# Attention weighed by pairs of heads with split operands, and a router on raw rows

## The chip, the cores and the metric

One core of one Trainium2 chip runs the whole program. The metric is the device time of one execution in microseconds (us). Its engines: TensorE (PE, with its weight loads as PEld), VectorE (DVE), ScalarE (ACT), GpSimd (POOL) and SyncE (SP, which here only issues transfers). They run their own instruction streams in order and meet at semaphores. SBUF is the working memory; PSUM, eight banks of 128 partitions x 512 fp32 values, takes the results of PE.

## The reference, cut to what matters

Four sequences of 256 rows of 256 values go through four sublayers, each added to its input:

```
x = x + graph_attention(ctx, adjacency = layernorm(x))      # 2 layers, 8 heads
x = x + sparse_mixture(layernorm(x))                        # 8 experts, top 2
x = x + learned_adjacency(ctx, layernorm(x))                # similarity, top 76 a row
x = x + block(x)                                            # below

# block: 32 query heads on 4 key/value heads of 128, then 32 experts (top 8) and a shared one
q, k, v = rope(h @ Wq), rope(h @ Wk), h @ Wv                # h = rmsnorm(x) * ln1
attn    = softmax(causal(q @ k.T / sqrt(128)))
x       = x + (attn @ v) @ Wo
x       = x + experts(rmsnorm(x) * ln2)

# router of the sparse mixture
logits = layernorm(x) @ w_router                            # 1024 rows x 8
weights, chosen = top_2(softmax(logits))
```

The change touches `attn @ v` and the router of the sparse mixture.

## The kernel before

Activations lie as eight tiles of 128 rows; a sequence is two of them. The stages follow one another on each engine: graph attention, router and ranking, sparse mixture over 23 tiles of 128 slots, learned adjacency, attention, expert mixture. Each engine's order is written out by hand; semaphores (`S[...]`) tie them.

**Attention.** 32 heads are taken in 8 blocks: block `blk` is key/value group `g = blk // 2` on one half (512 rows, two sequences). A block has ten projection jobs (values, keys, eight query heads), each 512 columns wide, at fixed iterations (`JOB_AT`), and 16 units: one query head of one sequence. Unit `u` is head `r`, sequence `b2` of `unit_of(u)`. Every engine runs `for k in range(FIRST, END)`, and in iteration `k` does its part for units at fixed lags:

- PE: `turn(k-2)`, three 128x128 transposes of the probabilities into `PT_BANK` (one bank); `scores(k+1)`; a job of `project` if there is one; `weigh(k-3)`, values times transposed probabilities into `O_BANK` (one bank), in fp32, 256 and 128 columns; `project_out(k-5)`, six fp32r products of 256 columns.
- ACT: `high_out(k-4)`, the rounded upper part of the weighed outputs into `o_ring`; `swap_halves` for the job of iteration `k-1`; `copy_T(k-2)`, from `PT_BANK` to `probT`; `exps(k)`; in some iterations upper parts of weights.
- DVE: `shift(k)` (mask and row minimum), `low_out(k-4)` (the remainder of the outputs), `normalise(k-1)`, `rotate` for the job of `k-2`, `cosines` for the job of `k-1` (for a values job: the copy to `vt`), and, from k = 6 to 13, `residual`. At k = 3 it splits the second half of the activations.
- POOL: the sine part of the rotation, lower parts of weights.

A product of two fp32 operands in *split* form is three fp32r products: upper x upper, upper x lower, lower x upper (`split_product`, L54). The projections and the output product are made so; the product with the values is not. An fp32 product shows as two records in the trace, an fp32r product as one.

**Router.** In the last iterations of the graph stage (`ALL` = 64, `LAST` = 77), for each sequence b: PE transposes the layer's output (`turn_x1`), DVE adds it to `xs` (`add_x1`) and takes mean and variance (`measure`), POOL makes the inverse root (`inverse`), DVE normalises into `norm` (`normalise_graph`), PE transposes that (`turn_graph`), ACT copies it to `actT` (`copy_graph`), PE multiplies with `wr0` into bank 2 (`route_graph`). `router0` on DVE then takes the row maximum, ACT the exponential, DVE the sum, the two largest of eight and the choice, over all eight tiles at once; PE counts ranks (`rank_slots`). SP stores the normalised rows to `x_rows` (`store_graph`), from which POOL gathers rows for the experts.

Of the kernel before, what the change touches and what calls it, by code (L numbers as in the profile page):

```python
# [14 lines left out]
P = 128  # L15
# [85 lines left out]
def build(nc, x, ctxT, W0, W1, a_self0, a_neigh0, a_self1, a_neigh1, b01,  # L101
          w_router, w_gate, w_up, w_down, WqT, WkT, gamma, ln1, ln2, Wq, Wk, Wv, Wo, Wr, ebias,
          Wg, Wu, Wd, ident_in, ind_in, rope_q, rope_k, causal_in, before_in, out):
    with ExitStack() as ctx:
# [12 lines left out]
        kv = sb("kv", [P, 2, B * N])  # L117
# [26 lines left out]
        route = sb("route", [P, 6, T, E1])  # L144
# [10 lines left out]
        kT = kv[:, 0, :]  # L155
        vt = kv[:, 1, :].rearrange("p (t n) -> p t n", t=T)
# [115 lines left out]
        def sb_resting(name, shape):  # L272
# [18 lines left out]
        probT = sb("probT", [P, 2, 3 * P])  # L291
# [6 lines left out]
        down_w = sb("down_w", [P, 2, I1 // P, D])  # L298

# [13 lines left out]

            "chosen_done", "earlier_done", "count_ready", "owner_done", "hot_done", "kind_done", "put_done", "place_done", "idx_ready", "idx_done", "rows_out",
# [18 lines left out]
            "s_ready", "s_shift", "p_exp", "p_inv", "p_norm", "pT_ready", "pT_copied",  # L333
# [16 lines left out]
        NORM_AT, TURN_AT, ROUTE_AT = (ALL, ALL + 2, ALL + 10), (ALL + 2, ALL + 4, ALL + 11), (ALL + 4, ALL + 6, ALL + 12)  # L350
# [34 lines left out]

        BLOCKS = 2 * KV
# [15 lines left out]

        def turn2_bank(t):

            return (Q_BANK[0], Q_BANK[1], bank[1], bank[3])[t // 2][:, t % 2 * D:t % 2 * D + D]
# [5 lines left out]
        def unit_of(u):  # L411

            blk, rem = divmod(u, BU)
            return (blk, blk // 2, blk % 2) + divmod(rem, 2)
# [34 lines left out]
        def _(sp):  # L449
# [107 lines left out]
        def _(pe):  # L557
# [25 lines left out]
            def graph_attention():  # L583
# [99 lines left out]
                def turn_graph(b):  # L683

                    pe.wait_ge(S["norm_done"], NT * b + NT)
# [4 lines left out]
                    for nt in range(NT):  # L690
                        for c in range(HC):
                            mm = pe.transpose(MISC[:, nt * D + c * P:nt * D + c * P + P],
                                              norm[:, NT * b + nt, c * P:c * P + P], ident[:])
                    mm.then_inc(S["normT_ready"], NT)

                def route_graph(b):

                    pe.wait_ge(S["normT_copied"], NT * b + NT)
                    if b == 0:
                        pe.wait_ge(S["const_in"], 16 * 5)  # L700
                        pe.wait_ge(S["z_copied"], ALL)
                    for t in range(NT * b, NT * b + NT):
                        for c in range(HC):
                            mm = pe.matmul(bank[2][:, t * E0:(t + 1) * E0], actT[:, c, t * P:t * P + P],
                                           wr0[:, c, :], start=c == 0, stop=c == HC - 1)
# [7 lines left out]
                for k in range(-1, LAST):  # L713
# [16 lines left out]
                    for b in range(B - 1):  # L730
                        if k == TURN_AT[b]:
                            turn_graph(b)
                        if k == ROUTE_AT[b]:
                            route_graph(b)
                turn_graph(B - 1)
# [1463 lines left out]
```

## Time and profile before

| | us |
|---|---|
| median of 3 runs | 1094.86 (1094.78 to 1096.74) |
| the profiled execution | 1095.35 |
| its span | 1093.5 |
| PE busy in the span | 1001.4 (92%) |
| PEld, DVE, ACT, POOL busy | 863.9, 870.9, 640.0, 431.6 |
| mean granted clock of PE | 0.945 of full speed |
| graph stage and router | about 0 to 192 |
| sparse mixture | about 206 to 338 |
| attention | about 366 to 830 |
| expert mixture | about 830 to 1093 |

The profile is of one execution. Matmuls are pipelined: a record's duration is longer than the time by which it holds up the next, so the distance between the ends of neighbouring records is the cost of one. The same holds for DVE and ACT, where the distance between starts is the cost and the duration tells when the result is there. A row of a timeline gives the start, the duration, engine, line, operation, output and inputs, and in brackets the idle time before it and what ended it. "By line" in the chain of waits is the share of the window that each line has in the chain that ended last.

### The profile page before, as it was taken

The page shows a single profiled execution, that of the slowest core. Times are in us where ns is not written, and L with a number is a line of the kernel's source. Part 1 is how long each engine was busy: PE and PEld are TensorE (multiplying, and loading weights), DVE is VectorE, ACT ScalarE, POOL GpSimd, SP SyncE. Part 2 cuts the span into 40 slices and gives each one's busy share as a digit, 9 for nine tenths or more (in the row PEclk, how much of TensorE's full clock was granted, in tenths as well). Part 3 has the DMA queues.
Part 4 walks back from the last instruction along what each step waited for, and adds up shares of the span by engine and source line. Part 5 has one row for each costly group of instructions (what it writes and reads, how often), then busy time and mean ns, then how long its engine had stood idle before and what let it go on. Part 6 is the DMA issues. An engine that isn't in the chain of part 4 may idle for free.

```text
span 1093.5 us, 21079 instructions
## 1 busy us (share of the span) xinstructions
PE 1001.4 (92%) x6394; PEld 863.9 (79%) x6394; DVE 870.9 (80%) x2644; ACT 640.0 (59%) x1767; POOL 431.6 (39%) x372
## 2 busy tenths in 40 slices
PE   4798777999994689999999999999989999999997
PEld 2455545799993478999999999999878888888886
DVE  6999997677765889777786777777878878788887
ACT  4789984655552387877777777777843222222221
POOL 5789893543321243323232333212422332232231
PEclk9869887699997599999999999999999999999999
DMA  9700003011115011010101100000000111111111
GB/s 291 256 1 2 1 2 108 29 55 49 47 37 172 2 39 50 1 40 2 49 2 39 35 2 2 1 2 1 26 20 30 44 43 58 43 43 49 52 43 38
DMA packets 49462, 49.30 MB, mean 45 GB/s; under 512 B 4896, under 2 KB 42464, under 8 KB 49376
## 3 DMA queue, kind: packets, MB, share of 16 engines
q1 hardware_dynamic: 45888, 40.83, 11.9%
q0 software_dynamic: 2208, 6.03, 1.9%
q10 hardware_dynamic: 1280, 1.38, 0.4%
q8 instruction: 43, 0.70, 0.3%
q14 instruction: 43, 0.35, 0.1%
HBM read 43.11 MB, written 5.11 MB: 44 GB/s over the span
## 4 chain that ended last, share of the span: by engine, by line
PE 72%; DVE 11%; POOL 7%; ACT 5%; issue 4%; DMA 1%; SPq 0%; DVEq 0%; ACTq 0%; POOLq 0%
PE bank L57 13%; PE bank L58 13%; PE bank L59 13%; PE bank L954 7%; PE bank L975 5%; PE bank L857 4%; PE bank L866 4%; PE bank L878 4%; PE bank L964 3%; POOL rest L1418 3%; PE bank L976 2%; POOL alpha L1421 2%; DVE alpha L1626 1%; PE bank L646 1%; PE bank L933 1%
## 5 line engine op out<-in xcount | busy, mean ns | idle before, releaser
L1483 POOL TENSOR_TENSOR rot_s<-swap,rq 128x512 f32<-128x512 f32 x64 | 88.6, 1385 | 194.7 <-ACT swap L1261 194.6
L1134 ACT ACTIVATE silu<-bank 128x512 f32<-128x512 f32 x66 | 39.4, 598 | 173.6 <-PE bank L59 173.6
L2073 DVE TENSOR_TENSOR o_ring<-bank,o_ring 128x256 fp32r<-128x256 f32 x128 | 54.2, 424 | 80.3 <-ACT o_ring L1290 78.9
L1274 ACT ACTIVATE prob<-prob,pmin 128x128 f32<-128x128 f32 (+1 forms) x256 | 113.3, 447 | 5.5 <-DVE pmin L2054 5.5
L954 PE MATMUL bank<-kv,norm 128*128 128x128 f32 (+1 forms) x512 | 105.8, 330 | 5.2 <-DVE norm L2047 5.2
L1896 DVE SCALAR_TENSOR_TENSOR xs<-bank,wt,xs 128x256 f32<-128x256 f32 x264 | 109.0, 476 | 0.1
L1439 POOL TENSOR_TENSOR gate_r<-gate_w,gate_r 128x256 fp32r<-128x256 f32 x31 | 36.4, 1174 | 177.3 <-ACT gate_r L1127 177.3
L1290 ACT ACTIVATE o_ring<-bank 128x256 fp32r<-128x256 f32 x128 | 48.3, 377 | 76.4 <-PE bank L976 76.3
L57 PE MATMUL bank<-wo_r,o_ring 128*128 128x256 f32 x256 | 82.4, 322 | 0.0
L1874 DVE TENSOR_TENSOR hidf<-silu,bank 128x512 f32<-128x512 f32 x66 | 45.4, 687 | 44.9 <-ACT silu L1134 43.3
L2066 DVE TENSOR_SCALAR prob<-prob,pinv 128x128 f32<-128x128 f32 (+1 forms) x256 | 77.0, 343 | 4.6
L2054 DVE CUSTOM_DVE_ANT_0 prob<-bank,causal 128x128 f32<-128x128 f32 (+1 forms) x256 | 80.1, 350 | 0.1
L975 PE MATMUL bank<-probT,kv 128*128 128x256 f32 x256 | 76.9, 382 | 3.3 <-DVE o_ring L2073 3.3
L1066 ACT ACTIVATE alpha<-alpha,edge_min 128x256 f32<-128x256 f32 x128 | 64.8, 527 | 19.1 <-DVE edge_min L1626 11.9
L57 PE MATMUL bank<-actT_r,wqk_r 128*128 128x512 f32 x144 | 72.3, 502 | 3.2 <-DVE kv L2020 3.2
L57 PE MATMUL bank<-down_r,hidT 128*128 128x256 f32 x248 | 70.2, 283 | 2.7 <-DVE xs L1896 1.4
L954 PEld LDWEIGHTS bank<-kv,norm 128*128 128x128 f32 x512 | 67.7, 193 | 6.2 <-DVE norm L2047 6.1
L59 PE MATMUL bank<-wo_r,o_ring 128*128 128x256 f32 x256 | 72.2, 282 | 0.0
L58 PE MATMUL bank<-wo_r,o_ring 128*128 128x256 f32 x256 | 72.0, 281 | 0.0
L1626 DVE CUSTOM_DVE_ANT_0 alpha<-alpha,norm 128x256 f32<-128x256 f32 x128 | 69.7, 580 | 2.6 <-POOL alpha L1421 2.2
L1284 ACT ACTIVATE probT<-bank 128x384 f32<-128x384 f32 x128 | 62.7, 490 | 13.7 <-PE bank L964 7.9
L59 PE MATMUL bank<-down_r,hidT 128*128 128x256 f32 x248 | 70.2, 283 | 0.0
(309 smaller groups left out, 3151.4 us busy)
## 6 DMA issues: line engine op xcount, KB each, us to landing
gate_w<-in_Wg SPq DMA_DIRECT2D x33, 128.0 KB, 2.2
up_w<-in_Wu SPq DMA_DIRECT2D x33, 128.0 KB, 2.3
down_w<-in_Wd SPq DMA_DIRECT2D x33, 128.0 KB, 2.3
w_all<-in_w_gate SPq DMA_DIRECT2D x8, 512.0 KB, 10.6
w_all<-in_w_up SPq DMA_DIRECT2D x8, 512.0 KB, 10.4
w_all<-in_w_down SPq DMA_DIRECT2D x8, 512.0 KB, 10.6
wq_g<-in_Wq SPq DMA_DIRECT2D x4, 1024.0 KB, 5.6
wo_g<-in_Wo SPq DMA_DIRECT2D x4, 1024.0 KB, 5.6
```

Source lines behind the costliest of these rows:

```text
L57: pe.matmul(out, lhs[0], rhs[0], start=first, stop=False)
L58: pe.matmul(out, lhs[0], rhs[1], start=False, stop=False)
L59: return pe.matmul(out, lhs[1], rhs[0], start=False, stop=last)
L954: mm = pe.matmul(S_BANK[u % 2][:, nt * P:nt * P + (nt + 1) * P], qT[:, (u // 2) % 4, b2 * N + nt * P:b2 * N + nt * P + P], kT[:, b * N:b * ...
L975: pe.matmul(O_BANK[:, 0:N], vt[:, t, :], probT[:, u % 2, 0:N], start=True, stop=False)
L1066: ins = act.activation(alpha[:, k % RING, nt * N:nt * N + N], alpha[:, k % RING, nt * N:nt * N + N], ACT.Exp, bias=edge_min[:, k % RING, n ...
L1274: ins = act.activation(prob[:, u % 4, nt * P:nt * P + (nt + 1) * P], prob[:, u % 4, nt * P:nt * P + (nt + 1) * P], ACT.Exp, bias=pmin[:, u ...
L1483: pool.tensor_tensor(rot_s[:, m % 2].rearrange("p (b n) -> p b n", b=2), swap[:, m % 2].rearrange("p (b n) -> p b n", b=2), bcast(tab[:, 1 ...
L1626: ins = dve.tensor_tensor_reduce(out=alpha[:, k % RING, nt * N:nt * N + N], in0=alpha[:, k % RING, nt * N:nt * N + N], in1=adj[:, r % B, n ...
L1896: ins = dve.scalar_tensor_tensor(xs[:, t, :], DB[2 * (mod % 2) + j // 2][:, j % 2 * D:j % 2 * D + D], w, xs[:, t, :], ALU.mult, ALU.add)
L2054: ins = dve.tensor_tensor_reduce(out=prob[:, u % 4, nt * P:nt * P + (nt + 1) * P], in0=S_BANK[u % 2][:, nt * P:nt * P + (nt + 1) * P], in1 ...
L2066: ins = dve.tensor_scalar(prob[:, u % 4, nt * P:nt * P + (nt + 1) * P], prob[:, u % 4, nt * P:nt * P + (nt + 1) * P], pinv[:, u % 4, nt:nt ...
```

## The change

**Attention.** `vt` and `probT` become fp32r, with the remainders `vt_low` and `probT_low` beside them. `unit_of` is reordered so that units 2p and 2p+1 are two heads of one sequence, which share their values. `weigh` takes a pair: three products of 512 columns (both heads, first 128 keys) and three of 256 (second 128 keys, rows 128 to 255 of both), all into the one `O_BANK`. It stands at the head of even iterations. DVE gets `low_T`, which reads `PT_BANK` again; `turn` waits for that instead of the copy. `high_out` and `low_out` take a pair each, in even iterations.

**Router.** PE transposes the raw rows `xs` and multiplies them with `wr0`, from which its column means have been subtracted (`router_means`, `wr_centred`); DVE multiplies the logits by the inverse deviation (`scaled_logits`). Six tiles (`LEAD`) are routed apart from the last two, whose logits go to bank 3. The last graph's `normalise_graph` goes behind the scan in `router0`, memsets go ahead of the last `add_x1`, and SP issues the first query and value loads ahead of the last `store_graph`.

```diff
-        NORM_AT, TURN_AT, ROUTE_AT = (ALL, ALL + 2, ALL + 10), (ALL + 2, ALL + 4, ALL + 11), (ALL + 4, ALL + 6, ALL + 12)
+        NORM_AT, TURN_AT, ROUTE_AT = (ALL, ALL + 2, ALL + 10), (ALL, ALL + 1, ALL + 7), (ALL + 2, ALL + 3, ALL + 8)
 def unit_of(u):
-            return (blk, blk // 2, blk % 2) + divmod(rem, 2)
+            return blk, blk // 2, blk % 2, rem // 4 * 2 + rem % 2, rem // 2 % 2
 # SP
+            load_queries(0)
+            load_values(0)
             store_graph(B - 1)
             sp.dma_start(rq[:], rope_q).then_inc(S["att_in"], 16)
             sp.dma_start(rk[:], rope_k).then_inc(S["att_in"], 16)
-            load_queries(0)
-            load_values(0)
 # PE, graph stage
                 def turn_graph(b):
-                    pe.wait_ge(S["norm_done"], NT * b + NT)
+                    pe.wait_ge(S["x1_added"], b + 1)
 ...
-                                              norm[:, NT * b + nt, c * P:c * P + P], ident[:])
+                                              xs[:, NT * b + nt, c * P:c * P + P], ident[:])
+                def router_means():
+                    pe.wait_ge(S["const_in"], 16 * 5)
+                    pe.wait_ge(S["mean_set"], 1)
+                    pe.wait_ge(S["z_copied"], ALL)
+                    for c in range(HC):
+                        mm = pe.matmul(bank[2][:, T * E0:(T + 1) * E0], work[:, 0:P], wr0[:, c, :], start=c == 0, stop=c == HC - 1)
+                    mm.then_inc(S["wr_mean"], 1)
 # PE, attention
                 def turn(u):
                     pe.wait_ge(S["p_norm"], u + 1)
                     if u >= 1:
-                        pe.wait_ge(S["pT_copied"], u)
+                        pe.wait_ge(S["pT_low"], u)
 ...
+                def weigh(p):
+                    blk, g, half, r, b2 = unit_of(2 * p)
                     t = NT * (2 * half + b2)
+                    pe.wait_ge(S["pT_low"], 2 * p + 2)
 ...
+                    if p >= 1:
+                        pe.wait_ge(S["o_copied"], p)
+                    dst = O_BANK.rearrange("p (u n) -> p u n", u=2)
+                    for nt in range(NT):
+                        rows, cols = slice(nt * P, N), slice(nt * N, nt * P + N)
+                        for i, (v, weights) in enumerate(((vt[:, t + nt, :], probT), (vt[:, t + nt, :], probT_low),
+                                                          (v_low(t + nt), probT))):
+                            mm = pe.matmul(dst[:, :, rows], v, weights[:, :, cols],
+                                           start=nt == 0 and i == 0, stop=nt == NT - 1 and i == 2)
+                    mm.then_inc(S["o_ready"], 1)
                 for k in range(FIRST, END):
+                    if k % 2 == 0 and 0 <= k - 4 < AU:
+                        weigh((k - 4) // 2)
                     if 0 <= k - 2 < AU:
                         turn(k - 2)
 ...
-                    if 0 <= k - 3 < AU:
-                        weigh(k - 3)
 # ACT, attention
+                def high_out(p):
+                    act.wait_ge(S["o_ready"], p + 1)
+                    if 2 * p + 2 > O_RING:
+                        act.wait_ge(S["o_used"], 2 * p + 2 - O_RING)
+                    act.activation(out_pair(p, 0), O_BANK.rearrange("p (u n) -> p u n", u=2), ACT.Copy
+                                   ).then_inc(S["o_high"], 1)
                 for k in range(FIRST, END):
-                    if 0 <= k - 4 < AU:
-                        high_out(k - 4)
+                    if k % 2 == 0 and 0 <= k - 4 < AU:
+                        high_out((k - 4) // 2)
                     if (q := job_in(k, 1)) is not None:
                         swap_halves(*q)
 # ACT, router
+            act.wait_ge(S["lead_max"], 1)
+            act.activation(route[:, 0, 0:LEAD, 0:E0], route[:, 0, 0:LEAD, 0:E0], ACT.Exp).then_inc(S["lead_exp"], 1)
 # DVE, router0
+                scaled_logits(slice(0, LEAD), bank[2][:, 0:LEAD * E0], S["lead_ready"], 2 * B - 1, S["lead_max"])
+                two_largest(slice(0, LEAD), S["lead_exp"])
+                scaled_logits(slice(LEAD, T), bank[3][:, 0:NT * E0], S["logit_ready"], 2 * B, S["rmax_done"])
+                two_largest(slice(LEAD, T), S["rexp_done"])
 ...
+                normalise_graph(B - 1)
                 dve.wait_ge(S["count_ready"], 1)
 # DVE, attention
+                        dve.tensor_copy(high, src).then_inc(S["v_high"], 1)
+                        dve.wait_ge(S["v_high"], blk + 1)
+                        dve.tensor_tensor(vt_low[:, 0:4, 4 * half:4 * half + 4, :].rearrange("p j t e -> p j (t e)"),
+                                          src, high.bitcast(F32), ALU.subtract).then_inc(S["q_taken"], 1)
 ...
+                def low_T(u):
+                    dve.wait_ge(S["pT_copied"], u + 1)
+                    dve.tensor_tensor(probT_low[:, u % 2, :], PT_BANK[:, 0:3 * P], probT[:, u % 2, :].bitcast(F32),
+                                      ALU.subtract).then_inc(S["pT_low"], 1)
 ...
                 for k in range(FIRST, END):
                     if 0 <= k < AU:
                         shift(k)
-                    if 0 <= k - 4 < AU:
-                        low_out(k - 4)
                     if 0 <= k - 1 < AU:
                         normalise(k - 1)
+                    if k % 2 == 0 and 0 <= k - 4 < AU:
+                        low_out((k - 4) // 2)
+                    if 0 <= k - 2 < AU:
+                        low_T(k - 2)
                     if (q := job_in(k, 2)) is not None:
                         rotate(*q)
```

## Rows read from the trace of the kernel before

**Rows 1.** Windows: start:end, length, busy us of each engine, granted clock, DMA.
```profile
80.00:162.00 82.00, 63.91 (x514) 41.08 (x516) 79.07 (x227) 74.69 (x242) 72.63 (x47) 0.89 0.01 1
...
391.00:398.00 7.00, 4.23 (x23) 3.31 (x23) 6.03 (x15) 5.23 (x18) 1.27 (x1) 1.00 0.23 78
...
413.50:465.40 51.90, 51.09 (x328) 46.17 (x329) 45.02 (x160) 40.33 (x119) 18.00 (x14) 1.00 0.08 26
...
517.33:569.24 51.91, 51.91 (x345) 47.89 (x344) 39.32 (x150) 40.26 (x120) 18.89 (x15) 1.00 0.08 26
```
**Rows 2.** Chain of waits, one block, 517.33 to 569.24: start, us, what.
```profile
by line: PE bank L954 20.7%; PE bank L57 15.4%; PE bank L59 15.4%; PE bank L58 15.3%; PE bank L975 13.3%; PE bank L964 10.1%; PE bank L976 6.8%; PE bank L933 3.4%
...
519.12 0.43 PE bank L975 x2
520.49 0.33 PE bank L964 x3
520.82 0.66 PE bank L954 x4
521.47 0.24 PE bank L57
...
522.86 0.43 PE bank L975 x2
...
525.21 0.43 PE bank L975 x2
```
**Rows 3.** Timeline of PE: the end of a projection, the end of weighing.
```profile
538.38 0.40 PE L59 MATMUL bank<-actT_r,wqk_r 128*128 128x512 f32 x1
...
539.05 0.38 PE L976 MATMUL bank<-probT,kv 128*128 128x128 f32 x2
```
**Rows 4.** Timeline of ACT in the same iteration.
```profile
539.47 0.38 ACT L1290 ACTIVATE o_ring<-bank 128x256 fp32r<-128x256 f32 x1 [1.34 <-PE bank L976]
539.87 0.59 ACT L1260 ACTIVATE swap<-bank 64x512 f32<-64x512 f32 x1
...
541.09 0.49 ACT L1284 ACTIVATE probT<-bank 128x384 f32<-128x384 f32 x1
541.48 0.39 ACT L1274 ACTIVATE prob<-prob,pmin 128x128 f32<-128x128 f32 x1
...
542.36 0.36 ACT L1290 ACTIVATE o_ring<-bank 128x256 fp32r<-128x256 f32 x1
```
**Rows 5.** Timeline of DVE, one iteration without idle time.
```profile
535.99 0.28 DVE L2054 CUSTOM_DVE_ANT_0 prob<-bank,causal 128x128 f32<-128x128 f32 x1
...
536.66 0.42 DVE L2073 TENSOR_TENSOR o_ring<-bank,o_ring 128x256 fp32r<-128x256 f32 x1
537.00 0.15 DVE L2063 RECIPROCAL pinv<-psum_ 128x2 f32<-128x2 f32 x1
...
537.66 0.69 DVE L2047 TENSOR_TENSOR norm<-rot_c,rot_s 128x512 f32<-128x512 f32 x1
538.26 0.28 DVE L2054 CUSTOM_DVE_ANT_0 prob<-bank,causal 128x128 f32<-128x128 f32 x1
```
**Rows 6.** Timelines of ACT and PE: a wait of the transposes early in attention.
```profile
393.03 0.49 ACT L1284 ACTIVATE probT<-bank 128x384 f32<-128x384 f32 x1
...
393.66 0.52 PE L964 MATMUL bank<-ident,prob 128*128 128x128 f32 x3 [1.80 <-ACT probT L1284]
```
**Rows 7.** Chain of waits, 160 to 210: the last graph's rows and the router.
```profile
179.77 0.70 DVE xs L1667
...
183.51 1.13 PE bank L692 x4
...
187.28 0.23 DVE rcol L1727
...
191.04 0.28 DVE marks L1742
...
192.54 3.62 PE bank L561 x4
```

More of the change, by code:

```diff
@@ L1703, in graph_attention @@
                         divide(j)
+                    for b in range(B - 1):
+                        if k == NORM_AT[b]:
+                            normalise_graph(b)
                     if (j := quad_at(k, 4)) is not None:
                         elu(j)
+                    if k == ROUTE_AT[0]:
+                        dve.wait_ge(S["wr_mean"], 1)
+                        dve.tensor_tensor(wr0[:], wr0[:], bcast(bank[2][:, T * E0:(T + 1) * E0], 1, HC), ALU.subtract
+                                          ).then_inc(S["wr_centred"], 1)
                     if (r := round_at(k, 20)) is not None:
+                        if r == 2 * B - 1:
+                            dve.wait_ge(S["g_elu"], QUADS * 2 * B)
+                            dve.memset(ones[:], 1.0)
+                            dve.memset(padded[:], -1.0)
+                            dve.memset(marks[:, :, T:], 0.0)
+                            chain.link(dve.memset(same_e[:], 1.0))
+                            dve.memset(same_e[:, :, 0:1], 0.0)
                         add_x1(r)
@@ L1709, in graph_attention @@
                         measure(r)
-                    for b in range(B - 1):
-                        if k == NORM_AT[b]:
-                            normalise_graph(b)
                 measure(2 * B - 1)
-                dve.memset(ones[:], 1.0)
-                dve.memset(padded[:], -1.0)
-                chain.link(dve.memset(marks[:, :, T:], 0.0))
-                chain.link(dve.memset(same_e[:], 1.0))
-                chain.link(dve.memset(same_e[:, :, 0:1], 0.0))
-                normalise_graph(B - 1)
@@ new lines, in scaled_logits @@
+            def scaled_logits(ts, logits, ready, rms, done):
+                R = route[:, 0, ts, 0:E0]
+                dve.wait_ge(ready, 1)
+                dve.wait_ge(S["x_rms"], rms)
+                chain.link(dve.tensor_tensor(R, logits.rearrange("p (t e) -> p t e", e=E0), bcast(rstd[:, ts], 2, E0), ALU.mult))
+                chain.link(dve.tensor_reduce(rcol[:, 0, ts], R, X, ALU.max))
+                dve.tensor_tensor(R, R, bcast(rcol[:, 0, ts], 2, E0), ALU.subtract).then_inc(done, 1)
@@ L1736, in router0, with two_largest @@
+            def two_largest(ts, ready):
+                R = route[:, 0, ts, 0:E0]
+                dve.wait_ge(ready, 1)
+                chain.link(dve.tensor_reduce(rcol[:, 1, ts], R, X, ALU.add))
+                chain.link(dve.reciprocal(rcol[:, 2, ts], rcol[:, 1, ts]))
+                chain.link(dve.tensor_tensor(padded[:, ts, 0:E0], R, bcast(rcol[:, 2, ts], 2, E0), ALU.mult))
+                for t in range(ts.start, ts.stop):
                     dve.max(rtop[:, t, :], padded[:, t, 0:8])
```

100 lines of the change are left out of this document (46 added, 54 removed).

## The prediction

> **What bounds the kernel now.** I read the windows first, then the chain of waits of one steady stretch, then the timelines of the four engines in it. In the window 517.33 to 569.24, one block of 16 units of attention, TensorE (PE) is busy 51.91 of 51.91 us [rows 1]: nothing else can set the pace there. The chain of waits of that block is PE alone, and its pieces give what each step costs at the end of the pipeline, which is what a consumer sees [rows 2]. From one product with the values to the next: 3.74 us in an iteration with a projection (519.12 to 522.86), 2.35 in one without (522.86 to 525.21). Inside: three transposes 0.33, four records of scores 0.66, a projection 6 x 0.233 = 1.40, weighing 0.43 and 6.8% of 51.91/16 = 0.22, together 0.65, and the six products with the output weights what is left up to 520.49, 0.72, so 0.12 each. A block has 9 query/key jobs of 1.40 and a value job of 1.78, on iterations 1, 2, 4, 5, 7, 9 (values), 10, 12, 13, 15 counted from the block's unit 0. Taken by twos: (0,1), (2,3), (6,7), (10,11), (14,15) 6.09 each, (8,9) 6.47, (4,5) and (12,13) 7.49, sum 51.9, as the window says.
>
> The other engines have room on average, VectorE (DVE) 39.3 and ScalarE (ACT) 40.3 us [rows 1]. What matters is where they wait. ACT stands idle 1.34 us before the copy of the weighed outputs [rows 4], until the last record of L976 ends at 539.43 [rows 3], and only then swaps the halves of a projection that had ended at 538.78 [rows 3]. The swap was ready and stood behind `high_out` in ACT's order.
>
> **The change, part by part.**
>
> *Cheaper weighing.* Two units had 2 x 0.65 = 1.30 us of fp32 products. Six fp32r products take their place, three of 512 columns and three of 256. The rows give 0.233 for 512 columns of fp32r and 0.12 for 256, each with a weight load of its own [rows 2]: 3 x 0.233 + 3 x 0.12 = 1.05. Saved 0.25 a pair, 64 pairs, 16 us, if PE keeps running. If the run of 256 columns with a step between heads cost as unpipelined a record as the longest here (0.40 and 0.28), the pair would be 2.0; the nearest rows are the pipelined ones, and I take 1.05.
>
> *New DVE work.* `low_T` subtracts 384 columns out of PSUM for every unit. From start to start 256 columns take 0.34 (536.66 to 537.00) and 512 take 0.60 (537.66 to 538.26) [rows 5], so 384 take about 0.48, done after 0.57. `low_out` goes from two of 0.34 to one of 0.60, and the value job gets a second pass of 0.6 and its wait. Per block +7.7 - 0.7 + 0.7 = +7.7 on 39.3, so 47.0 below 49.9 left for PE: enough on average. In the window 413.5 to 465.4, where the residuals ride along, DVE has 45.02 already [rows 1]; with 7.7 it is over PE's 49.9 by 2.8.
>
> *Where the waits go.* This decides it. `PT_BANK` is one bank. Before, `turn(u)` waited for ACT's copy of the unit before; now it waits for `low_T`, which is behind that copy and, in even iterations, behind `low_out`. And `weigh` moves from the middle of an iteration to the head of an even one, while ACT's iteration still begins with `high_out`. So ACT reaches `high_out`, waits for a product that PE has only just begun, and behind it on ACT are the swap of the last projection (1.22 us, 539.87 to 541.09), the copy `copy_T` (0.49) and the exponentials (0.88, 541.48 to 542.36) [rows 4]. I count from the end of PE's previous iteration, for an even iteration without a projection that follows one with it (0, 6, 8, 14 of a block):
> weigh done 1.05; ACT starts 0.04 later (539.43 to 539.47) [rows 3, 4], `high_out` of 512 columns 0.60 (a swap half of 512 columns takes 0.59) to 1.70; swap to 2.92; `copy_T` done 3.41; `low_T` from 3.44 to 4.01; PE restarts 0.14 after its release (393.52 to 393.66) [rows 6] at 4.15, and three transposes from a standstill take 0.52 [rows 6]: 4.67. Then scores 0.66, projection 1.40, outputs 0.72: 7.45. Before, this pair took 6.09: +1.37 for it, and PE, whose own next piece would have been at 2.76, stands for about 1.5 us.
> Pair (2,3): the even iteration has its own projection and covers the first wait nearly (PE is through at 4.16). In the odd one ACT does exponentials to 4.19, swap to 5.41, copy to 5.90; `low_T` 5.93 to 6.50; the next weigh starts at 6.64 and, from a standstill, ends 0.24 late, so 6.88: +0.79. Pair (10,11): nothing to swap in 10, but two value passes lengthen DVE: after them `shift` (0.67), `normalise` (0.66) (535.99 to 536.66, 537.00 to 537.66) [rows 5] and `low_T` of unit 9 end at 6.09, 6.47 in all: +0.38. Pairs (4,5) and (12,13) have projections in both halves, cover everything and gain 0.25.
> A block: 4 x 1.37 + 0.79 + 0.38 - 2 x 0.25 = +6.15, so 58.1 us.
> Over the whole of attention, even iterations 4 to 120: the first kind 30 times (41.1), the second and third 7 times each (5.5, 2.7), the fourth 15 times (-3.8): +45.5. The start is bound by DVE (391 to 398: PE 4.23 of 7.00 [rows 1]): two `low_T` before the activations are split, and the first pairs, +2, between 0 and 4. The residuals add under 1 beyond what that stretch loses already. After iteration 121 there are no swaps: +1, between -1 and 3.
>
> *Router.* The last graph's rows no longer have to be measured and normalised before they are transposed: from the end of the addition at 180.46 to the transposes at 183.51 [rows 7], 3.05 us. Logits at about 184.3, not 187.28. Six tiles' routing runs on DVE meanwhile (181.55 to about 185.1), two tiles' is left, some 2.5 of the 3.76 us that eight take (187.28 to 191.04): the choice stands at 187.6, 3.4 sooner. What is next late is PE's features of the similarity (3.62 at 192.54 [rows 7]) after the ranks, which moves as a whole, since the first of the two is done while DVE chooses. The normalisation goes under the wait for the ranks. Its store goes behind the query loads on SP's queue; the gather on POOL asks for it only when DVE and PE have made the row numbers, so those hide it; without that cover it would cost the time that the store takes, about 2 us. The exponentials of ACT come twice, 0.3 us, on the path once. New memsets and the centring of the weights (under 1 us) lie beside PE's transposes. -3.3, between -4.5 and 0.
>
> *Sum.* 45.5 + 2 + 1 - 3.3 = +45.2. The profiled execution took 1095.35, its span 1093.5, so 1.85 lie around the span; it is 0.49 over the median. 1095.35 + 45.2 - 0.5 gives 1140.
>
> **A page on this.** The Trainium skill, "Perfetto Trace Analysis", section "Optimizing Tensor Performance", has two rules that pull apart here: larger matmuls are more efficient where possible, which speaks for the pair; and independent groups should rotate through PSUM banks so that emptying one overlaps the next group's products, which speaks against holding the one transposes' bank through two readers. By the first alone the sum is 16 us off; by the second the wait at that bank is what counts, as I have it.
>
> **The rivals.**
> *PE stays the bound* (12%). If ACT and DVE deliver before PE asks, only the arithmetic counts: 64 x 0.25 = 16 and 3.3 for the router, 1095 - 19 = 1076. For it: PE at 51.91 of 51.91, ACT and DVE at three quarters [rows 1]. It decides if the transposes' bank is free 2.76 us after the iteration's start; my chain has it at 4.01, so 1.25 us of it would have to be wrong, more than any one term except the swap. The same page, "Identifying the Most-Contended Engine", takes the engine of highest occupancy as the one to relieve; that rule gives this result.
> *Only the bank's wait, not the swap* (3%). If the swap got through before the copy's wait bites, the chain is 1.22 shorter, 2.79 after the start, and PE stands about 0.3 a pair from the restart alone: the 0.25 is eaten, the router remains, 1092 to 1100, say 1097.
> *The clock gives way* (5%). PE would be busy 86% of a block. In 80 to 162 it was busy 78% and was granted 0.89 [rows 1]; PE's 49.9 us a block would grow by 12%, 6 us, 45 in all: 1185. Against it: 391 to 398, with a gap of 1.80 [rows 6] and PE busy 60%, had 1.00 [rows 1].
> *The stall as worked out* (80%): 1140, by itself 1125 to 1155; 0.1 us in each of some 45 stalls is 4.5, a start or end off by its bounds 4, the router 3.
>
> **How the numbers follow.** Out of the range I leave the first rival and the clock, 17%; it takes in the second rival and the stall with all its bounds: 1096 to 1158. A measurement of this kernel tells about 0.2% from no change, 2 us: faster 0.13 (the first rival and a piece of the second), same 0.02, slower 0.85.
>
> **What would show it.** A steady block of about 58 us, not 50; PE idle before the transposes of odd units, about 1.5 us, four times a block, released by DVE's `low_T`; in each, ACT idle before `high_out`, then swap, then copy, back to back; the idle of PE at weigh smaller and rarer; (4,5) and (12,13) without gaps, 7.24 us; clock 1.00; the choice of experts 3.4 us sooner. A steady block of 50 us would prove me wrong, as would idle that ends with `p_norm` (then DVE's load is the bound, not the order on ACT).

## The result, and the profile after

The changed kernel takes 1156.26 us, the median of 4 runs (1155.75 to 1166.4), where the kernel before takes 1094.82 beside it: a ratio of 1.0574, 95% interval 1.0545 to 1.0603. It is slower by 61.4 us; the forecast said slower by 45.2. Its range ended at 1158, so the time lies just inside; the part of it that belonged to the stall alone ended at 1155. One execution of the kernel before, among those beside the first four experiments, took 4046.8 us in the slow state and counts in no ratio below. The profiled execution has a span of 1154.0 us at a mean granted clock of 0.951, so 60.5 us more than before.

Line numbers move: in the kernel after, weighing is L1009, the transposes (`turn`) L993, scores L983, `high_out` L1324, the two halves of the swap L1294 and L1295, `copy_T` L1318, `low_T` L2129, `low_out` L2134, `normalise` L2122 and `rotate` L2103.

The windows first, as in [rows 1]: one steady block of 16 units, from its values job to the next one, and a longer stretch of attention. Columns are the busy times of PE, PEld, DVE, ACT and POOL with their instruction counts, the granted clock, the DMA share and GB/s.

```profile
535.85:595.74 59.89, 52.02 (x329) 45.91 (x328) 50.66 (x159) 39.85 (x112) 18.43 (x15) 1.00 0.07 23
476.49:776.00 299.51, 260.98 (x1633) 230.63 (x1632) 247.02 (x791) 196.24 (x550) 82.76 (x65) 0.99 0.05 16
```

A block has gone from 51.91 to 59.89 us, and PE, busy all of it before, now stands for 7.9. The clock is full in that block, but not in the whole stretch, as its mean of 0.99 says:

```profile
737.00:741.00 4.00, 4.00 (x15) 3.25 (x15) 3.76 (x17) 1.13 (x5) 0.00 (x0) 0.57 0.02 6
```

It stood at the lower of its two levels (half, 1.2 GHz) from 737.3 to 740.7, after a stretch, 715 to 735, in which PE was busy 18.60 of 20.00 us. The projection's products follow one another there at 0.43 us in place of 0.23, and the pair of iterations around it takes 9.44 us where the same pair of other blocks takes 7.87. That is 1.6 us of the loss in this profile. Why the clock fell there and nowhere else in this attention after 379 us is open. What PE waits for is in the view of its waits, over the whole run (us in total, times, longest):

```profile
PE bank L993 <- DVE probT_low L2129: 47.6, 35, 1.9
PE bank L1009 <- DVE probT_low L2129: 20.3, 24, 2.4
```

Here is one stall, an even iteration without a projection after an odd one with it, first on PE:

```profile
560.48 0.39 PE L1009 MATMUL bank<-probT,vt 128*128 128x512 f32 x1
...
561.41 0.28 PE L1009 MATMUL bank<-probT,vt_low 128*128 128x256 f32 x1
561.53 0.49 PE L993 MATMUL bank<-ident,prob 128*128 128x128 f32 x3
...
563.10 0.28 PE L59 MATMUL bank<-wo_r,o_ring 128*128 128x256 f32 x1
564.80 0.52 PE L993 MATMUL bank<-ident,prob 128*128 128x128 f32 x3 [1.41 <-DVE probT_low L2129]
```

then on ACT:

```profile
561.73 0.60 ACT L1324 ACTIVATE o_ring<-bank 128x512 fp32r<-128x512 f32 x1 [1.99 <-PE bank L1009]
562.35 0.59 ACT L1294 ACTIVATE swap<-bank 64x512 f32<-64x512 f32 x1
562.96 0.59 ACT L1295 ACTIVATE swap<-bank 64x512 f32<-64x512 f32 x1
563.57 0.49 ACT L1318 ACTIVATE probT<-bank 128x384 fp32r<-128x384 f32 x1
```

and on DVE:

```profile
562.36 0.69 DVE L2134 TENSOR_TENSOR o_ring<-bank,o_ring 128x512 fp32r<-128x512 f32 x1 [0.70 <-ACT o_ring L1324]
564.09 0.56 DVE L2129 TENSOR_TENSOR probT_low<-bank,probT 128x384 fp32r<-128x384 f32 x1 [1.04 <-ACT probT L1318]
```

The zero of the forecast's chain is the end of PE's previous iteration, here 560.64 (the output product of 560.36 took 0.28). From there the weighing is done at 1.05 (561.41 + 0.28 = 561.69), `high_out` at 1.69, the swap at 2.91, the copy at 3.42, and `low_T` runs from 3.45 to 4.01; PE restarts at 4.16. The forecast had 1.05, 1.70, 2.92, 3.41, 3.44 to 4.01 and 4.15. ACT had stood for 1.99 us ahead of `high_out`, with the swap ready, and the bank that it copies last had been full since 562.02. A second finding lies in rows of another kind, DVE and then POOL at one place:

```profile
603.10 1.54 DVE L2122 TENSOR_SCALAR prob<-prob,pinv 128x128 f32<-128x128 f32 x2
```

```profile
603.02 1.28 POOL L1520 TENSOR_TENSOR rot_s<-swap,rk 128x512 f32<-128x512 f32 x1
```

The two normalisations of a unit (x2) take 0.55 us at 561.10, and 1.54 here: GpSimd's product of the sines had begun 0.08 earlier and ends at 604.30, and they end 0.34 after it. In the text below this is called a collision. `low_T`, which reads one operand from PSUM, is not held up so. The one of the stall above began at 564.09, in the middle of a product of GpSimd, and took its usual 0.56; none of the 50 that began with GpSimd at work took longer:

```profile
563.62 1.27 POOL L1520 TENSOR_TENSOR rot_s<-swap,rq 128x512 f32<-128x512 f32 x1 [6.61 <-ACT swap L1295]
```

### The profile page after: what moved, and what is told of

The parts are those of the page before. It is cut to its first block, busy times and chain, and to the rows that moved or that the text cites. A ratio compares the mean times of both kernels' runs of the same rounds, so it can differ in the third digit from the quotient of the medians.

```text
span 1154.0 us, 20728 instructions
## 1 busy us (share of the span) xinstructions
PE 998.6 (87%) x6270; PEld 847.2 (73%) x6270; DVE 947.2 (82%) x2726; ACT 636.3 (55%) x1704; POOL 427.0 (37%) x372
## 3 DMA queue, kind: packets, MB, share of 16 engines
q10 hardware_dynamic: 1280, 1.38, 0.4%
## 4 chain that ended last, share of the span: by engine, by line
PE 58%; DVE 17%; ACT 11%; issue 7%; POOL 4%; DMA 1%; SPq 0%; DVEq 0%; ACTq 0%; POOLq 0%
PE bank L57 10%; PE bank L58 10%; PE bank L59 10%; PE bank L1009 6%; PE bank L886 4%; PE bank L895 4%; PE bank L907 3%; PE bank L983 3%; DVE probT_low L2129 3%; ACT swap L1294 2%; ACT swap L1295 2%; POOL rest L1455 2%; PE bank L993 2%; ACT probT L1318 2%; DVE prob L2122 1%
## 5 line engine op out<-in xcount | busy, mean ns | idle before, releaser
L1520 POOL TENSOR_TENSOR rot_s<-swap,rq 128x512 f32<-128x512 f32 x64 | 82.3, 1287 | 246.8 <-ACT swap L1295 246.8
L983 PE MATMUL bank<-kT,norm 128*128 128x128 f32 (+1 forms) x512 | 107.0, 332 | 6.5 <-DVE norm L2103 6.5
L1324 ACT ACTIVATE o_ring<-bank 128x512 fp32r<-128x512 f32 x64 | 38.2, 597 | 125.8 <-PE bank L1009 125.8
L2129 DVE TENSOR_TENSOR probT_low<-bank,probT 128x384 fp32r<-128x384 f32 x128 | 70.7, 552 | 43.4 <-ACT probT L1318 43.4
L993 PE MATMUL bank<-ident,prob 128*128 128x128 f32 x384 | 64.2, 276 | 48.1 <-DVE probT_low L2129 47.6
L2122 DVE TENSOR_SCALAR prob<-prob,pinv 128x128 f32<-128x128 f32 (+1 forms) x256 | 89.5, 392 | 4.6
L993 PEld LDWEIGHTS bank<-ident,prob 128*128 128x128 f32 x384 | 43.0, 141 | 57.1 <-issue 57.1
L983 PEld LDWEIGHTS bank<-kT,norm 128*128 128x128 f32 x512 | 67.6, 192 | 9.0 <-DVE norm L2103 8.6
L57 PE MATMUL bank<-down_r,hidT 128*128 128x256 f32 x248 | 70.2, 283 | 3.2 <-DVE xs L1949 1.9
L2134 DVE TENSOR_TENSOR o_ring<-bank,o_ring 128x512 fp32r<-128x512 f32 x64 | 44.1, 689 | 32.4 <-ACT o_ring L1324 32.4
```

Source lines behind the costliest of these rows:

```text
L57: pe.matmul(out, lhs[0], rhs[0], start=first, stop=False)
L983: mm = pe.matmul(S_BANK[u % 2][:, nt * P:nt * P + (nt + 1) * P], qT[:, (blk * REP + r) % 4, b2 * N + nt * P:b2 * N + nt * P + P], kT[:, b ...
L993: mm = pe.transpose(PT_BANK[:, j * P:j * P + P], prob[:, u % 4, j * P:j * P + P], ident[:])
L1520: pool.tensor_tensor(rot_s[:, m % 2].rearrange("p (b n) -> p b n", b=2), swap[:, m % 2].rearrange("p (b n) -> p b n", b=2), bcast(tab[:, 1 ...
L2122: ins = dve.tensor_scalar(prob[:, u % 4, nt * P:nt * P + (nt + 1) * P], prob[:, u % 4, nt * P:nt * P + (nt + 1) * P], pinv[:, u % 4, nt:nt ...
L2129: dve.tensor_tensor(probT_low[:, u % 2, :], PT_BANK[:, 0:3 * P], probT[:, u % 2, :].bitcast(F32), ALU.subtract).then_inc(S["pT_low"], 1)
```

## The experiments

Two theories stand against each other for the size of the loss. The first is the forecast's: ACT's order puts `high_out` and the swap ahead of the copy that frees the transposes' bank. The second is that `low_T` makes DVE late, whatever ACT's order; and under that a further question came up, whether DVE is late by the sum of its work or by collisions with GpSimd. "Block" below is the steady time from one values job to the next, read from the chain of waits: 51.9 before, 59.4 to 59.9 after (61.0 once, in the block with the clock's fall). The kernel before took 1094.8 to 1097.2 us on the chips used, so differences are taken from the one that ran beside.

**ACT's order.**

```diff
 # both_first: ACT; swap_first moves high_out only behind the swap
-                    if k % 2 == 0 and 0 <= k - 4 < AU:
-                        high_out((k - 4) // 2)
                     if (q := job_in(k, 1)) is not None:
                         swap_halves(*q)
                     if 0 <= k - 2 < AU:
                         copy_T(k - 2)
+                    if k % 2 == 0 and 0 <= k - 4 < AU:
+                        high_out((k - 4) // 2)
 # both_first: DVE, low_T ahead of low_out in the same way
```

> The changed kernel, but in even iterations ScalarE does the swap and the copy of the transposes before high_out, and VectorE does low_T before low_out. Theory (the order on ScalarE makes the stall): the wait of 1.41 us of TensorE before the odd unit's transposes, four times a block, falls to 0.1 to 0.2; a block goes from 59.4 to 51 to 53 us; the whole to 1095 to 1110. Rival (VectorE's added work is the bound): the order of the same instructions changes nothing, a block stays at 58 to 60, the whole at 1150 or more.

> The changed kernel with one line moved: ScalarE does the swap before high_out, nothing else. Theory: the chain is shorter by the swap, 1.22 us, so the wait of 1.41 falls to about 0.3 (restart included), a block to 54 or 55 us, the whole to 1115 to 1128. Rival (VectorE bound): no change, 1150 or more. Rival (the bank's second reader alone): waits of 1 us remain.

both_first took 1123.17 us beside 1096.57 before (ratio 1.0249, 1.0233 to 1.0265), with blocks of 55.2; swap_first 1124.11 (1.0261, 1.0245 to 1.0276). The loss falls from 61.4 us to 26.6 and 27.5: the order is worth 35 us, over half, and nearly all of it is had by letting the swap run while `high_out` would only wait. The stall itself is gone in both_first: from 476 to 740 us PE waits for the transposes' bank 4 times, at most 0.4 us, where the kernel after does 17 times for 1.4. In swap_first it waits 19 times there, for 0.3 to 0.7 us, more than the 0.3 expected, and DVE is busy 183.19 of 200. But both_first should have come to 1095 to 1110. PE now waits at the weighing, 12 times and 11.8 us in that stretch, released by `low_T`. In its windows DVE has become the busiest engine:

```profile
500.00:700.00 200.00, 188.22 (x1190) 167.42 (x1189) 190.76 (x576) 140.90 (x403) 63.95 (x50) 1.00 0.06 18
```

**What `low_T` costs in the changed kernel.** The lower part of the probabilities is left out: no `low_T`, and four products a pair in place of six.

```diff
-                        pe.wait_ge(S["pT_low"], u)
+                        pe.wait_ge(S["pT_copied"], u)
-                        for i, (v, weights) in enumerate(((vt[:, t + nt, :], probT), (vt[:, t + nt, :], probT_low),
-                                                          (v_low(t + nt), probT))):
+                        for i, (v, weights) in enumerate(((vt[:, t + nt, :], probT), (v_low(t + nt), probT))):
-                    if 0 <= k - 2 < AU:
-                        low_T(k - 2)
 # no_low_copy_first: the same, and ACT's order of both_first
```

> The changed kernel without the lower part of the probabilities: low_T and the two products with probT_low are left out, the transposes wait for ScalarE's copy alone. The order on ScalarE stays. Theory: the chain loses low_T (0.57 us) and one semaphore, so the wait of 1.41 becomes about 0.8 and stays, ended by ScalarE; the blocks take about 55. Rival (VectorE's added work is what costs): VectorE is back at its old load, the wait is gone, a block takes 49 us or less.

> As no_low (lower part of the probabilities left out), and ScalarE does the swap and the copy before high_out. Theory (two causes that add: the order on ScalarE, and low_T's load on VectorE): the four waits of 0.82 us a block go, a block falls from 51.6 to about 48, which is PE's own work (51.9 less 8 x 0.6), the whole from 1090 to about 1063. Rival (the order matters only together with low_T): stays at 1085 to 1090.

no_low took 1090.22 (one run) with blocks of 51.6, between the 55 and the 49 that the two theories gave; no_low_copy_first 1073.14 with blocks of 49.0, where 1063 and 48 were expected (before beside it 1096.39; ratio 0.9791, 0.9774 to 0.9807). The stall of the order is still in no_low, shorter by just what follows the copy. PE's timeline:

```profile
561.73 0.52 PE L993 MATMUL bank<-ident,prob 128*128 128x128 f32 x3 [0.82 <-ACT probT L1317]
```

The forecast's chain has `copy_T` done at 3.41 and `low_T` at 4.01, 0.60 later; the wait went from 1.41 to 0.82. Set against the kernel before beside each, the four kernels stand at +61.4 and +26.6 with `low_T`, -6.4 and -23.3 without. So the order costs 34.8 us with `low_T` and 16.9 without, and `low_T` with its products 67.8 in the order of the change and 49.9 in the other. Of these, two products a pair, 64 x (0.233 + 0.12) = 22.6 us, are PE's own by sum; no run left out only them. In the better order `low_T` still costs 27 us beyond that, which the forecast ("enough on average") did not have.

**Each part alone, on the kernel before.**

```diff
 # router_only: the kernel before with the router's part of the change
 # reorder_only: the kernel before with the new order of units
-            return (blk, blk // 2, blk % 2) + divmod(rem, 2)
+            return blk, blk // 2, blk % 2, rem // 4 * 2 + rem % 2, rem // 2 % 2
 # low_T_alone: the kernel before; probT_low is used by nobody
+                def low_T(u):
+                    dve.wait_ge(S["pT_copied"], u + 1)
+                    dve.tensor_tensor(probT_low[:, u % 2, :], PT_BANK[:, 0:3 * P], probT[:, u % 2, :],
+                                      ALU.subtract).then_inc(S["pT_low"], 1)
 # turn and the next copy_T wait for pT_low
```

> The kernel before with the router's part of the change alone (raw rows, centred weights, six tiles ahead). Expected 3.3 us less than before, 1091.5, as the first matmul of the sparse mixture stood at 203.32 in place of 206.62; the rest of the trace the same.

> The kernel before with the units taken two heads of one sequence after another, nothing else. Expected the same, 1095 to 1097: head 1 of a group of two is needed one unit sooner, which in the changed kernel showed as a wait of 0.17 us of the scores for the rotation in iteration 15. If it costs 3 us or more here, the reordering is a cause of its own.

> The kernel before with one thing added: VectorE's low_T for every unit (its result unused), and the transposes and the next copy wait for it. Units, products and order as before. Theory (low_T hurts where it stands in a chain with weigh at the head of an iteration; by load alone VectorE has 47 of 51.9 us): a block grows by 0 to 1.5 us, the whole 1095 to 1106. Rival (the added load and the bank held for two readers are enough): a block 54 or more, the whole over 1115.

router_only: 1092.65 beside 1096.57 (0.997, 0.9958 to 0.9983), so 3.9 faster; the mixture's first products of the experts come 3.3 us sooner in the changed kernel, at 203.32 in place of 206.62. reorder_only: 1098.05 beside 1096.39 in one run, blocks of 51.9: no change that it could tell. low_T_alone: 1127.46 beside 1096.39 (1.0283, 1.0266 to 1.03), blocks of 55.4. Here my expectation of 1095 to 1106 fell: one operation of 0.55 us more a unit, 128 x 0.48 = 61 us of DVE, cost 31 us in a kernel whose attention PE had bounded. In the window 500 to 700 DVE went from 152.2 to 178.4 of 200 busy, short of full, and PE from 200.0 to 191.9.

**Is it the load, or GpSimd?** GpSimd's product of the sines, 1.29 us, 8 query heads and the keys in a block, is cut to 16 of its 512 columns (0.23 us); the rest of it is left out (`rot_s` is set to zero once, ahead of attention).

```diff
-                pool.tensor_tensor(rot_s[:, m % 2].rearrange("p (b n) -> p b n", b=2),
-                                   swap[:, m % 2].rearrange("p (b n) -> p b n", b=2),
-                                   bcast(tab[:, 1, :], 1, 2), ALU.mult).then_inc(S["q_sin"], 1)
+                pool.tensor_tensor(rot_s[:, m % 2, 0:16], swap[:, m % 2, 0:16], tab[:, 1, 0:16], ALU.mult
+                                   ).then_inc(S["q_sin"], 1)
 # small_sines: in both_first; the others in the kernel before, in low_T_alone, in the kernel after
```

> As both_first, but GpSimd's sine products of the rotation cover 16 of 512 columns (the rest is left out), so that GpSimd is hardly ever at work beside VectorE. Theory (what is left over after the order is mended is VectorE's time, and part of that is normalise held up while GpSimd works: 1.5 to 1.9 us in place of 0.55): the waits at the pairs of iterations 4 and 10 shrink, a block goes from 55.3 to 53 or 54, the whole to 1108 to 1116. Rival (only the number of VectorE's instructions counts): no change from 1123.

> The kernel before, with GpSimd's product of the rotation's sines made on 16 of its 512 columns (the rest of that part is left out, so the rotation lacks most of its sine terms). A control: if TensorE is the bound throughout the attention of before, work taken from GpSimd, and any collision of it with VectorE, costs the end nothing: 1093 to 1097 us, blocks of 51.9 us. Rival: collisions of GpSimd with VectorE already cost before something: 5 us or more faster, blocks under 51.5 us.

> The kernel before with the one added operation of VectorE (the rest of the transposed probabilities, unused, for which the next turn waits), and GpSimd's product of the sines on 16 of 512 columns (the rest of that part is left out). The same without the smaller sines took 1127 us, with blocks of 55.4 us against 51.9. Theory: most of that 33 us is VectorE held up beside GpSimd's operations: 1098 to 1108 us, blocks of 52 to 53.3 us. Rival: it is VectorE's load and order by themselves: above 1118 us, blocks above 54.5 us.

> The changed kernel, with GpSimd's product of the sines on 16 of 512 columns (the rest of that part is left out). Theory: the stall of 1.41 us, four times a block, comes of ScalarE's order and stays; only what the forecast had missed goes (normalisations held up beside GpSimd, in the pairs 4 and 10 of a block, and part of the start): blocks of 58.0 to 58.8 us against 59.6, 1140 to 1149 us in all. Rival: the stall too rests on VectorE held up beside GpSimd: the wait of the turns falls below 0.8 us and the time below 1128 us.

| kernel | time (kernel before beside it) | block | the same with whole sines | block |
|---|---|---|---|---|
| before_small_sines | 1094.96 (1097.23) | 51.9 | 1097.23 | 51.9 |
| low_T_small_sines | 1103.72 (1097.23) | 52.3 | 1127.46 (1096.39) | 55.4 |
| small_sines | 1100.24 (1096.39) | 52.35 | 1123.17 (1096.57) | 55.2 |
| after_small_sines | 1139.48 (1097.23) | 57.97 | 1156.26 (1094.82) | 59.4 to 59.9, once 61.0 |

The four are single runs. Runs of one kernel differ by 1 to 3 us here, but for one of the kernel after, 10 above the others; the differences of 17 to 24 us are well clear of the 3. The control's 2.3 us is not, and its blocks of the steady stretch are unchanged. The one ahead of them, where the residuals ride along, takes 51.94 us against 53.79 in the kernel before: there GpSimd had already cost something (normalisations of 1.38 us at 420.26 and 1.40 at 430.61). small_sines came out faster than the 1108 to 1116 expected. Against the kernel before beside it, low_T_alone loses 31.1 us and low_T_small_sines 6.5, or 8.8 against its own control. So 22 to 25 of the 31 us went with the sines. The rest is load, order, and the lower parts of weights, which GpSimd still makes in full; no run parts these. A rival reading would be that shorter sines are merely ready sooner. The waits speak against it: through attention DVE waits for GpSimd's sines once, 0.7 us near the start, in low_T_alone, both_first and the kernel after alike, and PE and ACT never wait for them. DVE's lines of normalisation say the same, the 128x128 form in the kernel before, in both_first and in small_sines (busy, mean ns of one), one fence each:

```profile
L2066 DVE TENSOR_SCALAR prob<-prob,pinv 128x128 f32<-128x128 f32 x128 | 41.9, 328 | 4.6
```

```profile
L2122 DVE TENSOR_SCALAR prob<-prob,pinv 128x128 f32<-128x128 f32 x128 | 66.3, 518 | 4.6
```

```profile
L2122 DVE TENSOR_SCALAR prob<-prob,pinv 128x128 f32<-128x128 f32 x128 | 42.1, 329 | 4.6
```

With the 128x256 form (358, 499, 347 ns) both_first spends 44 us more on them than small_sines does, for the same instructions. In the kernel after, the stall stays where it was, so it is of ACT's order and not of GpSimd. PE's timeline in after_small_sines:

```profile
549.27 0.52 PE L993 MATMUL bank<-ident,prob 128*128 128x128 f32 x3 [1.42 <-DVE probT_low L2129]
```

**The sines on DVE.** If an operation of GpSimd costs DVE so much, DVE might as well do it.

```diff
 # DVE, cosines, in both_first; GpSimd's sines go
                                       bcast(tab[:, 0, :], 1, 2), ALU.mult).then_inc(S["q_taken"], 1)
+                    dve.tensor_tensor(rot_s[:, m % 2].rearrange("p (b n) -> p b n", b=2),
+                                      swap[:, m % 2].rearrange("p (b n) -> p b n", b=2),
+                                      bcast(tab[:, 1, :], 1, 2), ALU.mult).then_inc(S["q_sin"], 1)
```

> The changed kernel with the copy of the transposed probabilities ahead of the copy of the weighed outputs (as in both_first, 1123 us), and the product of the rotation's sines made by VectorE, right behind that of the cosines, instead of GpSimd. Nothing is left out. VectorE gets 9 operations a block, about 0.6 each, 5.4 us. Theory (an operation of GpSimd that VectorE runs into costs VectorE more than the operation itself would): blocks of 52.5 to 54 us against 55.3, 1098 to 1112 us. Rival (VectorE is the bound by the sum of its work, busy 191 of 200 us in both_first): the 5.4 us come on top, blocks above 56 us, 1135 us or more.

1122.71 beside 1096.83 (1.0238, 1.0221 to 1.0255), blocks of 55.1: both expectations missed, and the truth is between them. The time is that of both_first (1.0249) within the intervals. The normalisations are back at 317 and 347 ns, and in their place stand the sines:

```profile
L2085 DVE TENSOR_TENSOR rot_s<-swap,rq 128x512 f32<-128x512 f32 x64 | 47.3, 739 | 0.0
```

At 0.60 us from start to start (560.57 to 561.17), 72 of them occupy DVE for 43 us, about what the collisions had cost its normalisations. Giving them to GpSimd had relieved DVE of nothing, in this order of work.

## Why the prediction was right or wrong

**The sign and the mechanism held.** Slower, by PE's wait at the transposes' bank, because `high_out` waits for a product only just begun and the swap and the copy stand behind it. What was said to show it does: a wait of PE four times a block, released by `low_T`, 1.41 us against "about 1.5"; swap and copy back to back; the clock at 1.00 in a steady window. One sign did not come: (4,5) was to be without gaps. That the order is over half of the loss is shown by experiment.

**Pair by pair**, from weighing to weighing on PE's timeline (the forecast's numbers, then the kernel after, then after_small_sines):

| iterations of the block | before | forecast | after | after_small_sines |
|---|---|---|---|---|
| (0,1) and (6,7) | 6.09 | 7.45 | 7.42 to 7.54 | 7.44 |
| (2,3) | 6.09 | 6.88 | 6.83 | 6.83 |
| (4,5) | 7.49 | 7.24 | 7.57 to 7.97 | 7.33 |
| (8,9) | 6.47 | 7.83 | 7.83 | 7.83 |
| (10,11) | 6.09 | 6.47 | 7.08 | 6.10 |
| (12,13) | 7.49 | 7.24 | 7.33 | 7.32 |
| (14,15) | 6.09 | 7.45 | 7.87, once 9.44 | 7.67 |
| block | 51.9 | 58.1 | 59.4 to 59.9, once 61.0 | 57.97 |

Five of the eight pairs hold within 0.1 us. (10,11) and (4,5) are off where a normalisation meets GpSimd; one of 1.88 us at 580.31 is behind the 7.97. With the sines cut they fall to 6.10 and 7.33; so the 0.38 that the forecast had put on (10,11) for the second pass over the values was worth nothing by itself. In (14,15) another wait was missed: PE's scores wait 0.17 us for the rotated query of the next block (L983, for `rotate` behind the late `low_T`), and with the lost pace that is 0.2 with small sines and 0.4 without. The 0.24 us by which (2,3) let a weighing from a standstill end late stand in no row of the forecast; the trace has 0.10 (515.36 to 516.51, 1.15 against 1.05).

**The sum.** By places, against the forecast's terms (the times of the values jobs 465.42, 724.98 before; 476.49, 776.00 after; the ends of the spans):

| part | forecast | after | after_small_sines less its control |
|---|---|---|---|
| router | -3.3 | -3.3 | -3.3 (taken over) |
| attention up to iteration 25 | +10.6 | +14.4 | +11.1 |
| five blocks | +30.8 | +39.9 | +30.2 |
| the rest | +7.1 | +9.5 | +6.5 |
| sum | +45.2 | +60.5 | +44.5 |

The two columns of results are differences of times in the traces, the last row of spans. With the sines small in both kernels the change costs 44.5 us where 45.2 was forecast. That it comes so near is partly luck. The control's attention began late (its first values job at 357.78, 355.31 in the kernel before, behind a transfer of 5.42 us that took 2.94 there), and its clock was at half from 818.3 to 821.8. Counted from the first values job to the third, the change costs 14.6 us with whole sines and 14.2 with small ones (there with the clock at half from 388.7 to 392.1), where the forecast has 10.6. As far as two single traces tell, the start of attention was sized too low even without the collisions, and the control's delays hid it in the sum.

The surer comparison is the kernel after with and without whole sines: the span falls by 16.3 us, 5.3 of it up to iteration 25, 9.7 in the five blocks, 1.3 behind them. Of the 9.7, 1.6 are the clock's fall. Some 15 us are left, close to the 16 that the forecast lacked, and spread over all of attention: they are collisions with GpSimd. The durations agree: the means of the two normalisations and of `rotate` fall from 395, 388 and 809 ns to 337, 347 and 714, which is 19 us of DVE over 128, 128 and 64 of them.

**The step that failed** is "new DVE work", and in it the sentence "47.0 below 49.9 left for PE: enough on average". The count was right: in the window 500 to 700 of after_small_sines DVE is busy 163.12 of 200, that is 47.3 in a block of 57.97, against the 47.0 of the forecast. With whole sines it is 166.42, 49.6 in a block of 59.64; in the block shown above 50.66. The surplus is longer operations, not more of them. I had taken the normalisation's time from [rows 5] as if it belonged to the instruction (0.66 with the reciprocal). It depends on where GpSimd stands, and on which of the two began first. In the kernel before they meet three times in a steady block, but there `rotate` has begun and it is GpSimd that takes longer, here beside a `rotate` from 534.78 to 535.47:

```profile
535.05 1.57 POOL L1483 TENSOR_TENSOR rot_s<-swap,rq 128x512 f32<-128x512 f32 x1 [2.42 <-ACT swap L1261]
```

That costs DVE nothing: its normalisations have means of 328 and 358 ns, against 319 and 351 with the sines small, and `rotate` 715 against 701. The change shifts DVE's work so that GpSimd is often the first. The trace of before did hold the price, in the block that I read, in one normalisation on DVE and one lower part of weights on POOL:

```profile
517.67 0.86 DVE L2066 TENSOR_SCALAR prob<-prob,pinv 128x128 f32<-128x128 f32 x2
...
520.75 0.55 DVE L2066 TENSOR_SCALAR prob<-prob,pinv 128x128 f32<-128x128 f32 x2
```

```profile
516.91 1.27 POOL L1457 TENSOR_TENSOR wqk_r<-wq_g,wqk_r 128x512 fp32r<-128x512 f32 x1 [0.62 <-ACT wqk_r L1248]
```

GpSimd is through at 518.18, and the normalisations that began at 517.67 take 0.86 where the next take 0.55. I read GpSimd only as an engine with time to spare, and not as one that holds up another.

The Trainium skill, "SBUF — State Buffer", section "Who interferes with whom", has the rule that I should have weighed: VectorE and GpSimd share a port pair by an exclusive lock, and a VectorE operation in one of the two-port modes (`tensor_scalar` can enter them), or with two inputs in SBUF, fully blocks while an operation of GpSimd that started first (and, for the second kind, reads SBUF) holds it; one with at most one SBUF input, outside those modes, does not contend. The trace agrees in all three: the normalisations of 1.54 us beside GpSimd's 1.28; `rotate`, both inputs in SBUF, 0.68 by itself, 1.05 us where it began at 638.85 with GpSimd busy from 638.62 to 639.35, and 1.75 at 383.16 with GpSimd busy from 383.06 to 384.37 (both end 0.55 after GpSimd does); `low_T`, one input in PSUM, 0.56 at 564.09 with GpSimd at work.

**The rivals.** "PE stays the bound" needed the bank free at 2.76; it was free at 4.01. Its price of the weighing was sound (six products in 1.05 us, 560.48 to 561.53), its condition was not met. No run has all six products and PE as the bound: small_sines comes nearest, with blocks of 52.35 against the 49.9 of the sum, and no_low_copy_first, at 49.0, has only four products a pair. "Only the bank's wait, not the swap" gave 1092 to 1100; swap_first, which takes the swap out of the chain, gives 1124, since DVE is late next: that price forgot it. The clock did not give way as that rival had it: PE was busy 52.02 of 59.89 at 1.00, and the one fall cost 1.6 us, not 45.

**The router** gave 3.3 us as summed, with the choice of experts at 187.61 where 187.6 was forecast, and 3.9 by the runs of router_only. It is the one part of the change that is a gain by itself at full precision. no_low_copy_first is the fastest of all, 2.1% faster than before, at the price of the probabilities' lower part.

## What to carry to other kernels

When a wait is moved to the head of an iteration, list what is ready and stands behind it on that engine: here a swap and a copy, 1.7 us, behind a product just begun, and putting the ready work first won back 35 of 61 us. When an operation is added to an engine that has "time to spare on average", read that engine's durations beside GpSimd's timeline first: the `tensor_scalar` here and the sum of two SBUF operands stretched by up to a microsecond where GpSimd had begun first, and which begins first depends on the order that the change itself alters. Look for it from GpSimd's side too: a product that takes 1.57 us in place of 1.27 is a collision that the other engine has won. Cut the suspected neighbour to a few columns, in the changed kernel and in the unchanged one: the two together give its share of the loss. Then compare the traces place by place, and read the clock in each: two totals can agree by chance.

## What the runs showed of the hardware

- A GpSimd product of 512 columns mostly takes 1.27 to 1.30 us. Where it had begun first, it held up VectorE's normalisations by about 1 us (a pair of 0.55 took 1.54). Where VectorE's `rotate` had begun first, GpSimd was the one held up: in the kernel before, all 21 products that began during a `rotate` between 400 and 830 us took 1.56 to 1.58, and `rotate` its usual 0.68 to 0.69.
- Moving that product to VectorE (0.60 us each) left the whole kernel's time as it was: 1.0238 of the kernel before, against 1.0249 without the move.
- fp32r products whose 256 columns lie in two runs with a step between them went through at 0.12 us each, like unbroken ones (561.17 to 561.53 for three); the bound of 2.0 us a pair, which the forecast kept for the case that they did not, was not needed.
